# Interleaving the experts' hidden rows so that one gate tile serves a whole chunk, with new orders of work on every engine

## The chip, the cores and the metric

The kernel runs on one core of a Trainium2 chip. The time is the device time of one execution in microseconds (us). The kernel before was timed three times: 297.48, 299.65 and 299.68 us, median 299.65 us. The execution that the profiler recorded took 301.82 us, of which 300.0 us lie between the first and the last instruction.

## The reference, cut to what matters

There are 2048 tokens of 128 channels (4 batches of 512). Two layers follow each other, each a cross-attention and a feed-forward part, all with residuals. The first feed-forward part sends each token to one of 8 experts. The change lies in the second one, which computes every expert for every token:

```python
combine = zeros((n, E)).at[arange(n)[:, None], tidx].add(tw)   # n = 2048, E = 16, 4 of 16 are not zero
g = einsum('nh,eih->nei', x, w1)                  # I = 96 hidden values per expert
u = einsum('nh,eih->nei', x, w3)
hact = silu(g) * u * combine[:, :, None]          # the gate of a token and expert scales 96 hidden values
y = einsum('nei,ehi->nh', hact, w2)               # summed over experts and hidden values
shared = einsum('ni,hi->nh', silu(x @ ws1.T) * (x @ ws3.T), ws2)
return y + shared
```

The 16 x 96 = 1536 hidden values may stand in any order, as long as w1, w3, w2 and the gates use the same one.

## The kernel before, in words

Every engine walks its own list of stages, written out by hand in `ORDER`, an item `stage:n` at a time; semaphores between engines are the only other thing that sets the order. `a.` are the stages of the first attention and its router (chunks 0 to 3 of 512 tokens), `t.` the tiles of 128 tokens sorted by expert (11 tiles of the first group, chunk 0, then 19 of the second, chunks 1 to 3), `w.` the preparation of weights, and names without a prefix are the second attention and the second feed-forward part. `FILL` puts matmuls whose result nobody reads (`warm_b`, 512 columns) in front of some stages on PE.

The second feed-forward part works in blocks. For each of 4 chunks there are 13 blocks (`N1`), 12 of 128 hidden rows and one, the shared expert, of 96. `block(n)` maps the running number n to chunk c and block r; `SHARED` says at which r the shared expert stands. One block is:

- PE `g` and `u`: three 512-column matmuls each (high and low halves of a split product), into bank 0 and bank 1
- PE `e`: one matmul of the selection matrix `sel1` with the transposed gates `gT`, which spreads the 16 gates over the block's 128 hidden rows, into bank 3 (not for the shared block)
- ACT `silu` (L808) of bank 0 into `act`; DVE `prod` (L1300) act times bank 1; DVE `hm` (L1317) times bank 3 (the shared block takes bank 1 directly)
- ACT `high` (L814) rounds hm into `hring`; POOL `low` (L950) makes the remainder `lring`; PE `y` adds three matmuls to bank 2

`act`, `hm`, `hring` and `lring` have four places each. At the end of a chunk ACT `outcopy` takes bank 2 out, PE `oturn` transposes it, DVE `addout` adds it to x, and SP stores the chunk.

The gates of a chunk come from DVE `route0` to `route7`, some 35 small instructions on 128x64 values. `route7` writes gates as a high and a low half (L1272, L1274, L1275), PE `gturn` (L1615) transposes them to 32 rows, ACT `gcopy` (L802) writes them into `gT`. Both `gT` and `sel1` need zeros below row 32: POOL `clear` (L918, L919) writes them, after which ACT `sel` (L739) rounds `sel1` from a buffer that a DMA of 192 KB on ACT's queue filled at the start.

Between the sorted tiles and the blocks stand, for chunk 0: PE `wo`, DVE `add` with the statistics of the third norm, POOL `rstd3`, DVE `norm3`, PE `turn3`, PE `logit`, ACT `sg`, DVE `route`. For chunk 1 POOL `fetch:4` to `fetch:7` bring back the sorted rows by indirect DMA, then DVE `combine:1` with statistics, POOL `rstd2:1`, ACT `norm2:1`, PE `turn2:1`, `q:1`, `score:1`.

Of the kernel before, what the change touches and what calls it, by code (L numbers as in the profile page):

```python
# [1748 lines left out]
```

## Time and profile before

| | value |
|---|---|
| median of 3 runs | 299.65 us |
| profiled execution | 301.82 us, span 300.0 us |
| PE busy | 264.1 us (88%) |
| DVE, ACT, POOL busy | 192.8, 164.2, 151.6 us |
| mean granted TensorE clock | 0.975 |

A row of the timeline gives start and duration in us, the engine, the line, the operation with output and input tiles, and how many instructions are merged in it; in brackets is the idle time just before it and what ended it. Matmuls overlap, so the distance between two starts tells what one costs, not its duration. A row of the windows gives, for each engine, busy us and the number of instructions, then the granted clock.

### The profile page before, as it was taken

How to read it: one execution, taken by the hardware profiler on the slowest of the kernel's cores; microseconds unless marked ns; L12 is line 12 of the kernel's file. 1: busy time of each engine (PE TensorE's matmuls, PEld its weight loads, DVE VectorE, ACT ScalarE, POOL GpSimd, SP SyncE). 2: the span in 40 equal slices, each digit the busy share in tenths (PEclk: the TensorE clock that was granted, in tenths of full speed). 3: DMA queues.
4: the chain of work that ended last, by engine and by line, in shares of the span. 5: the costliest groups of instructions: out<-in, count | busy, mean ns of one | idle time of the engine just before them, and what ended most of it. 6: DMA issues, size and time to landing. Idle time of an engine off the chain costs nothing.

```text
span 300.0 us, 5426 instructions
## 1 busy us (share of the span) xinstructions
PE 264.1 (88%) x1712; PEld 197.4 (66%) x1719; DVE 192.8 (64%) x626; ACT 164.2 (55%) x325; POOL 151.6 (51%) x170
## 2 busy tenths in 40 slices
PE   8999966786679898649999999999899999999993
PEld 8787646675557654415667757776587876887871
DVE  5686655534284354696678888678695689755660
ACT  2745438352435740643866796677347864555441
POOL 2532876403259114854775923580556536655551
PEclk9999989799999999897999999999999999999999
DMA  7992262455553020100000000001000000000000
GB/s 240 363 378 118 86 218 74 112 137 148 154 138 93 19 63 9 28 9 16 27 13 9 2 0 2 2 0 37 0 2 1 1 35 2 1 0 35 2 1 35
DMA packets 19518, 19.60 MB, mean 65 GB/s; under 512 B 2194, under 2 KB 17154, under 8 KB 19234
## 3 DMA queue, kind: packets, MB, share of 16 engines
q1 hardware_dynamic: 13856, 14.41, 15.0%
q10 hardware_dynamic: 4610, 2.74, 3.1%
q0 software_dynamic: 1024, 2.10, 2.3%
q8 instruction: 14, 0.23, 0.3%
q14 instruction: 14, 0.11, 0.1%
HBM read 13.48 MB, written 5.77 MB: 64 GB/s over the span
## 4 chain that ended last, share of the span: by engine, by line
PE 39%; issue 23%; POOL 21%; DVE 10%; ACT 4%; another core or an unknown queue 1%; POOLq 1%; DVEq 0%; ACTq 0%
PE bank L1338 35%; POOL lring L950 11%; POOL gu1l L895 2%; PE bank L1350 2%; POOL rstd L855 2%; DVE sg L1222 1%; DVE st L974 1%; POOL rstd L850 1%; POOL w2l L901 1%; ACT xn L659 1%; DVE mpad L1186 1%; DVE xn L991 1%; ACT L808 1%; DVE x L1169 1%
## 5 line engine op out<-in xcount | busy, mean ns | idle before, releaser
L950 POOL TENSOR_TENSOR lring<-hm,hring 128x512 fp32r<-128x512 f32 (+1 forms) x52 | 66.5, 1290 | 63.1 <-ACT hring L814 63.1
L808 ACT ACTIVATE act<-bank 128x512 f32<-128x512 f32 (+1 forms) x52 | 31.0, 597 | 39.0 <-PE bank L1338 38.9
L1338 PE MATMUL bank<-xTh,gu1h 128*128 128x512 f32 (+1 forms) x104 | 45.2, 435 | 3.2 <-POOL xTl L861 2.5
L1300 DVE TENSOR_TENSOR act<-act,bank 128x512 f32<-128x512 f32 x48 | 32.9, 686 | 21.7 <-PE bank L1338 19.1
L1317 DVE TENSOR_TENSOR hm<-act,bank 128x512 f32<-128x512 f32 (+1 forms) x52 | 35.6, 684 | 12.9 <-PE bank L1338 9.3
L1338 PE MATMUL bank<-xTh,gu1l 128*128 128x512 f32 (+1 forms) x104 | 41.7, 401 | 0.0
L1338 PE MATMUL bank<-xTl,gu1h 128*128 128x512 f32 (+1 forms) x104 | 41.3, 397 | 0.0
L814 ACT CAST hring<-hm 128x512 fp32r<-128x512 f32 (+1 forms) x52 | 31.7, 617 | 10.6 <-DVE hm L1317 10.2
L747 ACT ACTIVATE hT<-bank,w 128x128 f32<-128x128 f32 x60 | 18.3, 364 | 22.3 <-PE bank L1338 22.0
L1338 PE MATMUL bank<-w,hT 128*128 x120 | 21.2, 301 | 10.6 <-DVE ys L1146 9.4
L1338 PEld LDWEIGHTS bank<-xTh,gu1h 128*128 128x128 f32 (+1 forms) x104 | 19.6, 189 | 13.8 <-issue 4.2
L659 ACT ACTIVATE xn<-x,shift_of,rstd 128x128 f32<-128x128 f32 x48 | 19.8, 483 | 14.9 <-POOL shift_of L857 14.9
L1338 PEld LDWEIGHTS bank<-w,hT 128*128 128x128 f32 x120 | 16.4, 198 | 16.2 <-issue 16.1
L1146 DVE TENSOR_TENSOR ys<-bank,b 128x128 f32<-128x128 f32 x30 | 8.7, 290 | 24.5 <-PE bank L1338 20.6
L1338 PEld LDWEIGHTS bank<-xTh,gu1l 128*128 128x128 f32 (+1 forms) x104 | 19.6, 188 | 4.9
L1338 PEld LDWEIGHTS bank<-xTl,gu1h 128*128 128x128 f32 (+1 forms) x104 | 19.8, 191 | 3.9 <-issue 0.6
L1338 PE MATMUL bank<-hring,w2h 128*128 128x512 f32 (+1 forms) x52 | 21.2, 407 | 1.0 <-POOL lring L950 1.0
L1338 PE MATMUL bank<-warm_b,onesb 128*128 128x512 bf16 x68 | 19.7, 381 | 1.6 <-issue 1.5
L1338 PE MATMUL bank<-hring,w2l 128*128 128x512 f32 (+1 forms) x52 | 20.5, 394 | 0.0
L1338 PE MATMUL bank<-lring,w2h 128*128 128x512 f32 (+1 forms) x52 | 20.4, 393 | 0.0
L1338 PE MATMUL bank<-xsT,w 128*128 128x128 f32 x120 | 19.6, 295 | 0.9 <-DVE xsT L1141 0.4
L1338 PE MATMUL bank<-gT,sel 128*128 128x512 f32 x48 | 19.5, 406 | 0.5 <-DVE hm L1317 0.4
(233 smaller groups left out, 522.6 us busy)
## 6 DMA issues: line engine op xcount, KB each, us to landing
w<-in_w SPq DMA_DIRECT2D x30, 129.0 KB
wf<-in_gu SPq DMA_DIRECT2D x1, 1632.0 KB, 9.3
xs<-sorted_x SPq DMA_DIRECT2D x19, 64.0 KB
sorted_y<-ys ACTq DMA_DIRECT2D x9, 128.0 KB, 2.1
x<-in_x SPq DMA_DIRECT2D x4, 256.0 KB, 5.2
w<-in_w SPq DMA_DIRECT2D x1, 1024.0 KB, 10.0
out_x<-x SPq DMA_DIRECT2D x4, 256.0 KB, 2.0
w<-in_w SPq DMA_DIRECT2D x1, 768.0 KB, 8.3
```

The lines of the kernel that those rows point to most:

```text
L659: nc.scalar.activation(normal(k, b)[:, j, :], x[:, b * TPB + j, :], ACT.Identity, bias=shift_of[:, ln(k, b), j:j + 1], scale=rstd[:, ln(k, ...
L747: last = nc.scalar.activation(hT0[:, t % 2, k, :], h_bank(t)[:, k * P:(k + 1) * P], ACT.Gelu, bias=b1_tile[:, t % SLOTS0, k:k + 1])
L808: nc.scalar.activation(act[0:m, n % 4, :], bank[0][0:m, :], ACT.Silu).then_inc(s.act_ready1, 1)
L814: nc.scalar.copy(hring[0:m, n % 4, :], hm[0:m, n % 4, :]).then_inc(s.hmh_ready, 1)
L855: nc.gpsimd.tensor_tensor(rstd[:, own, :], ve[:, own, :], mhalf[:, 0:TPB], ALU.pow).then_inc(s.ln_step[k], 1)
L895: nc.gpsimd.tensor_tensor(gu1l[:, w, own], gu1f[:, w, own], gu1h[:, w, own].bitcast(F32), ALU.subtract).then_inc(s.gul_ready, 1)
L950: nc.gpsimd.tensor_tensor(lring[0:m, n % 4, :], hm[0:m, n % 4, :], hring[0:m, n % 4, :].bitcast(F32), ALU.subtract).then_inc(s.hml_ready, 1)
L1146: nc.vector.tensor_tensor(ys[:, y_slot(t), :], y_bank(t)[:, 0:C], b2_0[:, bass.ds(own_expert[t], 1), :].rearrange("p o c -> p (o c)"), ALU ...
L1300: nc.vector.tensor_tensor(act[:, n % 4, :], act[:, n % 4, :], bank[1][:, :], ALU.mult).then_inc(s.prod_ready1, 1)
L1317: nc.vector.tensor_tensor(hm[0:m, n % 4, :], act[0:m, n % 4, :], bank[1 if r == SHARED[c] else 3][0:m, :], ALU.mult).then_inc(s.hm_ready1, 1)
L1338: return nc.tensor.matmul(dst, lhsT, rhs, start=start, stop=stop, skip_group_check=True)
L1350: last = nc.tensor.transpose(quarters(n)[:, j, :], normal(k, b)[:, j, :], ident)
```

## The change

The hidden rows of the 16 experts are interleaved on the host (`hidden`): block r now holds rows 8r to 8r+7 of every expert, so the gate of partition p is that of expert p // 8 in all 12 blocks. `route7` writes the gates of a chunk once, each repeated 8 times along the free axis (128x512), and `gturn` transposes that straight into bank 3, where it stays for the chunk. `sel1`, `gT`, the stages `e`, `gcopy`, `sel`, `clear` and the load of the selection matrix are gone. `gturn` of chunk n waits until all `hm` of the chunk before have read bank 3; the first `hm` with gates waits for it. The shared block comes first in every chunk. `oturn` moves from bank 3 to banks 2, 2, 4, 5, and where bank 2 is used the next chunk's first `y` also waits for `addout`. The statistics count one semaphore step instead of four. `t.h:11` waits for as many of the two late key products as stand up to `b.Vd`. SP's program has the same text and the same sequence as before: the second group's first five weight loads were already issued ahead of its rows.

```diff
-SHARED = (0, 4, 4, 4)
+SHARED = (0, 0, 0, 0)
...
-        "add:0 norm3:0 route0:0 combine:1 route1:0 route2:0 route3:0 route4:0 route5:0 route6:0 route7:0 hm:0 "
...
+        "add:0 norm3:0 route0:0 combine:1 hm:0 route1:0 route2:0 route3:0 prod:1 route4:0 route5:0 route6:0 "
...
+    "wo:0": 2,
+    "turn3:0": 12,
+    "logit:0": 2,
+    "g:0": 5,
+    "g:1": 3,
+    "u:1": 1,
+    "turn2:1": 6,
+    "q:1": 2,
...
-    "t.xs:11": 4,
-    "wo:0": 11,
-    "turn3:0": 15,
-    "logit:0": 2,
-    "g:0": 2,
-    "turn2:1": 8,
-    "score:1": 2,
...
-        gate1 = sb("gate1", [P, NT, 2, E1], F32R)
+        gate1 = sb("gate1", [P, TPB, E1, P // E1])
...
-        GATE_BANK = (3, 5, 5, 5)
+        OUT_BANK = (2, 2, 4, 5)
...
-            act_e.dma_start(sel1f, a["sel1"]).then_inc(s.ld_sel, 16)
...
-                elif stage == "clear":
-                    stored(NP)
-                    nc.gpsimd.memset(gT[:, :].bitcast(F32), 0.0).then_inc(s.cleared, 1)
-                    nc.gpsimd.memset(sel1[:, :, :].bitcast(F32), 0.0).then_inc(s.cleared, 1)
...
                 elif piece == 7:
-                    step(nc.vector.tensor_tensor(ra[:, t, :], ra[:, t, :], over(thr[:, t], E1), ALU.mult))
-                    step(nc.vector.tensor_copy(gate1[:, t, 0, :], ra[:, t, :]))
-                    nc.vector.tensor_tensor(gate1[:, t, 1, :], ra[:, t, :], gate1[:, t, 0, :].bitcast(F32),
-                                            ALU.subtract).then_inc(s.gate1_ready, 1)
+                    c = t0 // TPB
+                    if c:
+                        v.wait_ge(s.gT1_mm, c)
+                    nc.vector.tensor_tensor(gate1[:, :, :, :], ra[:, t, :].unsqueeze(3).broadcast_to([P, n, E1, P // E1]),
+                                            thr[:, t].unsqueeze(2).unsqueeze(3).broadcast_to([P, n, E1, P // E1]),
+                                            ALU.mult).then_inc(s.gate1_ready, 1)
...
                         v.wait_ge(s.prod_ready1, gated + 1)
-                        v.wait_ge(s.e_ready1, gated + 1)
+                        v.wait_ge(s.gT1_mm, c + 1)
...
-                        pe.wait_ge(s.kblk_ready, 2)
+                        pe.wait_ge(s.kblk_ready, [stage for stage, _ in order("DVE") if stage in ("b.Kd", "b.Vd")].index("b.Vd") + 1)
...
                     else:
-                        pe.wait_ge(s.at1_ready, 6 * min(n + 2, B))
+                        pe.wait_ge(s.hm_ready1, n * N1)
                     pe.wait_ge(s.gate1_ready, n + 1)
                     for j in range(TPB):
-                        last = nc.tensor.transpose(quarters(GATE_BANK[n])[0:2 * E1, j, :],
+                        last = nc.tensor.transpose(quarters(3)[:, j, :], gate1[:, j, :, :].rearrange("p e i -> p (e i)"), ident)
...
-                elif stage == "e":
...
-                    mm(bank[3][:, :], sel1[:, own, :], chunk(gT, c)).then_inc(s.e_ready1, 1)
...
                         pe.wait_ge(s.outT_ready, c)
+                        if OUT_BANK[c - 1] == 2:
+                            pe.wait_ge(s.o_added1, c)
...
+    def hidden(w):
+        return np.asarray(w).reshape(E1, R1, P // E1, C).transpose(1, 0, 2, 3).reshape(E1 * I1, C)
```

How the new tables move work is shown at three places. The first is PE where the sorted tiles end and the blocks begin, from `wo:0` (the first row with `aT`) on; `warm_b` rows are fills, `xTh` and `xTl` rows are `g` and `u`, `xn` rows transposes. Before:

```order
L1338 MATMUL bank<-warm_b,onesb 128x512 x11
L1338 MATMUL bank<-pack_b,aT 128x128 x4
L1338 MATMUL bank<-warm_b,onesb 128x512 x15
L1350 MATMUL bank<-pack_a,xn 128x128 x4
L1338 MATMUL bank<-warm_b,onesb 128x512 x2
L1338 MATMUL bank<-R1w,xT 128x128 x4
```

and after it, from the end of `g:1` to `u:1`:

```order
L1338 MATMUL bank<-warm_b,onesb 128x512 x8
L1350 MATMUL bank<-pack_a,xn 128x128 x4
L1338 MATMUL bank<-xT,pack_b 128x512
L1615 MATMUL bank<-pack_a,gate 32x128 x4
L1338 MATMUL bank<-xTh,gu1h 128x512
```

Now the same two pieces read:

```order
L1313 MATMUL bank<-warm_b,onesb 128x512 x2
L1313 MATMUL bank<-pack_b,aT 128x128 x4
L1313 MATMUL bank<-warm_b,onesb 128x512 x12
L1325 MATMUL bank<-pack_a,xn 128x128 x4
L1313 MATMUL bank<-warm_b,onesb 128x512 x2
L1313 MATMUL bank<-R1w,xT 128x128 x4
```

```order
L1313 MATMUL bank<-warm_b,onesb 128x512 x6
L1325 MATMUL bank<-pack_a,xn 128x128 x4
L1313 MATMUL bank<-warm_b,onesb 128x512 x2
L1313 MATMUL bank<-xT,pack_b 128x512
L1313 MATMUL bank<-xTh,gu1h 128x512
L1313 MATMUL bank<-xTl,gu1h 128x512
L1313 MATMUL bank<-xTh,gu1l 128x512
L1313 MATMUL bank<-maskrow,onesb 128x512 x4
L1313 MATMUL bank<-Kd,qT 128x128 x16
L1586 MATMUL bank<-pack_a,gate 128x128 x4
```

Nine of the 11 fills ahead of `wo:0` are gone. `u:1` now stands ahead of `turn2:1`, and `g:2` and `score:1` ahead of `gturn:0`.

The second place is POOL at the same time, after `rstd3:0` and the four fetches. Before:

```order
L873 DMA xn<-sorted_y,home 128x128 x4
L861 TENSOR_TENSOR xTl<-xT,xTh 128x512
L918 MEMSET gT 128x2048
L919 MEMSET sel 128x1536
L852 TENSOR_SCALAR ve<-mv 128x4
```

Now:

```order
L853 DMA xn<-sorted_y,home 128x128 x4
L841 TENSOR_TENSOR xTl<-xT,xTh 128x512
L832 TENSOR_SCALAR ve<-mv 128x4
L833 TENSOR_SCALAR nm<-mv 128x4
L835 TENSOR_TENSOR rstd<-ve,mhalf 128x4
```

The two memsets between `lowx:0` and `rstd2:1` are gone.

The third place is POOL in the first attention, behind `a.rstd2:0`. Before:

```order
L850 TENSOR_TENSOR rstd<-ve,mhalf 128x4
L852 TENSOR_SCALAR ve<-mv 128x4
L853 TENSOR_SCALAR nm<-mv 128x4
L855 TENSOR_TENSOR rstd<-ve,mhalf 128x4
L857 TENSOR_TENSOR shift_of<-nm,rstd 128x4
```

Now:

```order
L830 TENSOR_TENSOR rstd<-ve,mhalf 128x4
L900 TENSOR_SCALAR maskrow<-mask 128x512
L902 TENSOR_SCALAR keyoff<-maskT 128x4
L832 TENSOR_SCALAR ve<-mv 128x4
L833 TENSOR_SCALAR nm<-mv 128x4
```

`w.mask` came here from among the preparations of weights during the second group of tiles.

## Rows read from the trace of the kernel before

**Rows 1.** The page, busy time and share of the span of each engine.
```profile
PE 264.1 (88%) x1712; PEld 197.4 (66%) x1719; DVE 192.8 (64%) x626; ACT 164.2 (55%) x325; POOL 151.6 (51%) x170
```

**Rows 2.** Windows by stage: sorted tiles, first blocks, blocks beside attention, blocks alone.
```profile
44.00:110.00 66.00, 51.11 (x411) 41.42 (x410) 30.91 (x117) 34.79 (x87) 26.97 (x28) 0.96 0.39 109
124.00:138.00 14.00, 9.48 (x27) 4.69 (x29) 12.53 (x49) 5.65 (x10) 7.14 (x9) 0.76 0.04 11
138.00:250.00 112.00, 109.52 (x730) 79.80 (x729) 85.44 (x241) 75.92 (x133) 62.45 (x64) 1.00 0.03 9
250.00:290.00 40.00, 39.40 (x175) 31.15 (x173) 26.25 (x48) 20.11 (x35) 21.80 (x18) 1.00 0.02 7
```

**Rows 3.** Timeline, PE in the last chunk: from one block's g to the next.
```profile
279.00 0.40 PE L1338 MATMUL bank<-xTh,gu1h 128*128 128x512 f32 x1
279.69 0.39 PE L1338 MATMUL bank<-gT,sel 128*128 128x512 f32 x1
279.93 0.40 PE L1338 MATMUL bank<-xTh,gu1h 128*128 128x512 f32 x1
281.31 0.40 PE L1338 MATMUL bank<-xTh,gu1h 128*128 128x512 f32 x1
```

**Rows 4.** The page's costliest groups: busy us, mean ns of one, idle before, releaser.
```profile
L950 POOL TENSOR_TENSOR lring<-hm,hring 128x512 fp32r<-128x512 f32 (+1 forms) x52 | 66.5, 1290 | 63.1 <-ACT hring L814 63.1
L1300 DVE TENSOR_TENSOR act<-act,bank 128x512 f32<-128x512 f32 x48 | 32.9, 686 | 21.7 <-PE bank L1338 19.1
L1317 DVE TENSOR_TENSOR hm<-act,bank 128x512 f32<-128x512 f32 (+1 forms) x52 | 35.6, 684 | 12.9 <-PE bank L1338 9.3
L1338 PE MATMUL bank<-gT,sel 128*128 128x512 f32 x48 | 19.5, 406 | 0.5 <-DVE hm L1317 0.4
```

**Rows 5.** Timeline, passage: the end of the attention of chunk 0.
```profile
109.97 0.88 DVE L1204 TENSOR_TENSOR aT<-aT,bank 128x128 f32<-128x128 f32 x4
110.85 2.32 PE L1338 MATMUL bank<-warm_b,onesb 128*128 128x512 bf16 x10
113.01 1.05 PE L1338 MATMUL bank<-pack_b,aT 128*128 128x128 f32 x8
```

**Rows 6.** Timeline, first blocks: the last fetch, the clears, sg, combine, turn2.
```profile
121.57 0.94 POOL L873 DMA_INDIRECT xn<-sorted_y,home  x1 [0.30 <-issue]
122.90 4.03 DVE L1222 TENSOR_SCALAR sg<-sg 128x64 f32<-128x64 f32 x1 [4.13 <-issue]
123.73 1.83 POOL L918 MEMSET gT<- 128x2048 f32 x1
125.48 1.40 POOL L919 MEMSET sel<- 128x1536 f32 x1
127.81 1.14 DVE L1169 SCALAR_TENSOR_TENSOR x<-xn,score,x 128x128 f32<-128x128 f32 x4
133.00 1.39 PE L1350 MATMUL bank<-pack_a,xn 128*128 128x128 f32 x4 [3.43 <-ACT xn L659]
```

**Rows 7.** DMA issues: line engine op xcount, median us to landing.
```profile
xn<-first_sorted_y,slot POOLq DMA_INDIRECT x4, 2.9
```

**Rows 8.** Timeline, first blocks: first and last of route1 to route7.
```profile
130.19 0.16 DVE L1227 TENSOR_TENSOR pr<-sbs 128x32 f32<-128x32 f32 x1
136.67 0.22 DVE L1275 TENSOR_TENSOR gate<-route,gate 128x64 fp32r<-128x64 f32 x1
```

**Rows 9.** Timeline: a two-input DVE instruction beside POOL's low; the key product.
```profile
250.50 1.29 POOL L950 TENSOR_TENSOR lring<-hm,hring 128x512 fp32r<-128x512 f32 x1 [0.33 <-ACT hring L814]
250.55 1.32 DVE L1255 TENSOR_TENSOR route<-route,top 128x64 f32<-128x64 f32 x1
70.99 0.68 DVE L1154 TENSOR_TENSOR Kd<-kT,pack_b 128x512 f32<-128x512 f32 x1
```

**Rows 10.** Timeline: the same four norm instructions, POOL free and POOL busy.
```profile
20.91 1.11 DVE L991 TENSOR_SCALAR xn<-x,mv,rstd 128x128 f32<-128x128 f32 x4 [0.60 <-POOL rstd L850]
87.39 2.18 DVE L991 TENSOR_SCALAR xn<-x,mv,rstd 128x128 f32<-128x128 f32 x4
```

More of the change, by code:

```diff
@@ L162 @@
     "a.score:1": 1,
-    "a.own:0": 1,
     "a.wturn:0": 1,
@@ L167 @@
     "a.wturn:1": 1,
+    "a.turn:3": 1,
     "a.score:2": 1,
+    "a.turn2:0": 2,
     "a.own:1": 1,
+    "a.logit:0": 1,
     "a.mix:1": 1,
-    "a.turn2:0": 1,
     "a.wturn:2": 1,
-    "a.logit:0": 1,
+    "a.rank:0": 1,
     "a.own:2": 1,
-    "a.rank:0": 1,
+    "a.place:0": 1,
     "a.mix:2": 1,
-    "a.turn:3": 1,
-    "a.place:0": 1,
+    "a.score:3": 1,
     "a.turn2:1": 1,
-    "a.score:3": 1,
-    "a.logit:1": 1,
     "a.own:3": 1,
     "a.wturn:3": 1,
+    "a.logit:1": 1,
+    "a.mix:3": 1,
     "a.rank:1": 1,
-    "a.mix:3": 1,
-    "a.turn2:2": 2,
-    "a.logit:2": 3,
-    "t.xs:0": 2,
-    "t.xs:11": 4,
-    "wo:0": 11,
-    "turn3:0": 15,
-    "logit:0": 2,
-    "g:0": 2,
-    "turn2:1": 8,
-    "score:1": 2,
+    "a.turn2:2": 1,
+    "t.xs:0": 2,
+    "wo:0": 2,
[6 more added lines that the diff above has]
+    "q:1": 2,
+    "a.logit:2": 3,
 }
@@ L230, in xattn_moe_kernel @@
         xTl = sb("xTl", [C, NT * P], F32R)
-        gT = sb("gT", [P, NT * P], F32R)
-        sel1 = sb("sel1", [P, R1, P], F32R)
+        sb("early_only", [P, NT * P + R1 * P])
         (attn0, s0, kT0, vT0, A0, bqrep, aT0, V0, z0, m0, rk0, oh0, over0, past0, jump0, ones) = shared_room([
@@ L358, in xattn_moe_kernel @@
         hm = sb("hm", [P, 4, 512])
-        sel1f = hm[0:2 * E1, :, :].rearrange("p a n -> p (a n)")[:, 0:R1 * P].rearrange("p (r n) -> p r n", r=R1)
         outT = xT[:, 2, :]
@@ L372, in xattn_moe_kernel @@
         s.ld_tab = sem("ld_tab")
-        s.ld_sel = sem("ld_sel")
         s.ld_mask = sem("ld_mask")
@@ L401, in xattn_moe_kernel @@
         s.gul_ready = sem("gul_ready")
-        s.cleared = sem("cleared")
-        s.sel_ready = sem("sel_ready")
         s.s0_mm = sem("s0_mm")
@@ L476, in xattn_moe_kernel @@
         s.fetched0 = [sem(f"fetched_first{t}") for t in range(TPB - 1)]
-        s.ln_stats = [sem(f"ln_stats{k}") for k in range(4)]
         s.ln_var = [sem(f"ln_var{k}") for k in range(4)]
@@ L735, in weights @@
                     round_w2(n)
-                elif stage == "sel":
-                    act_e.wait_ge(s.ld_sel, 16)
-                    act_e.wait_ge(s.cleared, 2)
-                    nc.scalar.copy(sel1[0:2 * E1, :, :], sel1f).then_inc(s.sel_ready, 1)
             def sorted_tile(stage, t):
@@ L797, in stage1 @@
                     nc.scalar.activation(tiles(sg, n), tiles(sg, n), ACT.Exp, scale=-1.0).then_inc(s.sg_ready, 1)
-                elif stage == "gcopy":
-                    act_e.wait_ge(s.gT1_mm, n + 1)
-                    if n == 0:
-                        act_e.wait_ge(s.cleared, 1)
-                    nc.scalar.copy(chunk(gT, n)[0:2 * E1], bank[GATE_BANK[n]][0:2 * E1, :]).then_inc(s.gT1_ready, 1)
                 elif stage == "silu":
@@ L973, in statistics @@
                 for j in range(TPB):
-                    nc.vector.bn_stats(st[:, own, j, :], xc[:, j, :]).then_inc(s.ln_stats[k], 1)
-                v.wait_ge(s.ln_stats[k], TPB * (b + 1))
+                    last = nc.vector.bn_stats(st[:, own, j, :], xc[:, j, :])
+                step(last)
                 aggregate(k, b)
@@ L1172, in combine @@
                         v.wait_ge(s.x2_ready, t + 1)
-                        nc.vector.bn_stats(st[:, ln(2, 0), t, :], x[:, t, :]).then_inc(s.ln_stats[2], 1)
+                        last = nc.vector.bn_stats(st[:, ln(2, 0), t, :], x[:, t, :])
                 if b == 0:
-                    v.wait_ge(s.ln_stats[2], TPB)
+                    step(last)
                     aggregate(2, 0)
@@ L1308, in stage1 @@
                         v.wait_ge(s.hml_ready, n - 3)
-                    if n == 0:
-                        v.wait_ge(s.sel_ready, 1)
                     if r == SHARED[c]:
@@ L1320, in stage1 @@
                     v.wait_ge(s.out_mm, n + 1)
-                    nc.vector.tensor_tensor(tiles(x, n), tiles(x, n), quarters(3), ALU.add).then_inc(s.o_added1, 1)
+                    nc.vector.tensor_tensor(tiles(x, n), tiles(x, n), quarters(OUT_BANK[n]), ALU.add).then_inc(s.o_added1, 1)
             for stage, n in order("DVE"):
@@ L1543, in stage1 @@
                     pe.wait_ge(s.xT_ready[2], n + 1)
-                    if n == 3:
-                        pe.wait_ge(s.gT1_ready, 2)
                     mm(bank[5][:, :], attn1_w[:, 1, :], xT[:, xT_slot(2, n), :]).then_inc(s.q_mm, 1)
@@ L1637, in stage1 @@
                         .then_inc(s.u_mm if w else s.g_mm, 1)
-                elif stage == "e":
-                    c, r, own, m, gated = block(n)
-                    if gated == c * R1:
-                        pe.wait_ge(s.gT1_ready, c + 1)
-                    if gated == 0:
-                        pe.wait_ge(s.sel_ready, 1)
-                    else:
-                        pe.wait_ge(s.hm_ready1, n - 1 if r - 1 == SHARED[c] else n)
-                    if c and r == SHARED[c] + 1:
-                        pe.wait_ge(s.o_added1, c)
-                    mm(bank[3][:, :], sel1[:, own, :], chunk(gT, c)).then_inc(s.e_ready1, 1)
                 elif stage == "y":
@@ L1661, in stage1 @@
                     pe.wait_ge(s.outT_ready, n + 1)
-                    pe.wait_ge(s.hm_ready1, (n + 1) * N1 + SHARED[n + 1] if n < B - 1 else B * N1)
+                    if OUT_BANK[n] != 2:
+                        pe.wait_ge(s.at1_ready, 6 * B)
                     for j in range(TPB):
-                        last = nc.tensor.transpose(quarters(3)[:, j, :], cut(outT, j), ident)
+                        last = nc.tensor.transpose(quarters(OUT_BANK[n])[:, j, :], cut(outT, j), ident)
                     last.then_inc(s.out_mm, 1)
@@ L1731 @@
         "maskT": np.tile(np.asarray(mask_BxS2_bf0).T, (HG, 1)),
-        "sel1": np.tile(np.repeat(np.eye(E1, dtype=np.float32), I1, axis=1), (2, 1)).reshape(2 * E1, R1, P),
         "w1_0": np.concatenate([np.asarray(L0_ffn_W1), np.asarray(L0_ffn_b1).reshape(E0, HID0, P).transpose(0, 2, 1)], axis=2),
@@ L1735 @@
         "b2_0": np.asarray(L0_ffn_b2).reshape(1, E0, C),
-        "gu1": up(*(np.concatenate([np.asarray(w).reshape(E1 * I1, C), np.asarray(sw)]).T
+        "gu1": up(*(np.concatenate([hidden(w), np.asarray(sw)]).T
                     for w, sw in ((L1_ffn_w1, L1_ffn_ws1), (L1_ffn_w3, L1_ffn_ws3)))),
-        "w2_1": np.asarray(L1_ffn_w2).transpose(0, 2, 1).reshape(R1, P, C).transpose(1, 0, 2),
+        "w2_1": hidden(np.asarray(L1_ffn_w2).transpose(0, 2, 1)).reshape(R1, P, C).transpose(1, 0, 2),
         "ws2": np.asarray(L1_ffn_ws2).T,
```

5 lines of the change are left out of this document (removed), and 148 rows, old and new, of the table ORDER.

## The prediction

> **What bounds the kernel now.** I read the busy shares first: PE is busy 88% of the span, no other engine above 64% [rows 1]. An average hides stages, so the windows come next [rows 2]. From 138 to 250 us (blocks beside the second attention of chunks 1 to 3) and from 250 to 290 us (blocks alone) PE is busy 109.52 of 112 us and 39.40 of 40 us at full clock, DVE 85.4 and 26.3 us. In these 152 us what leaves PE shortens the run, as long as DVE, ACT and POOL keep up. The window before is another matter: from 124 to 138 us PE is busy 9.5 of 14 us, partly with fills, and the granted clock averages 0.76, so part of it ran at 1.2 instead of 2.4 GHz. From wo:0 to there the passage from sorted tiles to blocks is a chain through all engines, and its latency counts. From 44 to 110 us PE is busy 51 of 66 us; that stage waits from step to step.
>
> In the last chunk the same block returns every 281.31 - 279.00 = 2.31 us, ten matmuls, and `e` takes 279.93 - 279.69 = 0.24 us of it [rows 3]. Its listed 0.406 us [rows 4] contains the overlap with its neighbour and is not its price. The ten together give 0.231 us each, which I use.
>
> **The change, part by part.**
>
> 1. *48 `e` matmuls leave PE*: 48 x 0.231 = **-11.1 us**. A block falls to 2.08 us of PE. Against that stand per block on DVE 0.686 + 0.684 = 1.37 us and on POOL 1.29 us [rows 4]; both fit. The 16 transposes of the gates stay 16.
>
> 2. *Nine fills ahead of `wo:0` leave*. aT is complete at 110.85, just when the fills begin, and `wo` starts at 113.01; ten merged fills take 2.32 us, the last overlapping [rows 5]. The distance from 110.85 to 113.01 is 2.16 us for ten, 0.216 each, so nine give **-1.9 us**. DVE `add`, `norm3` and the fetches stand behind `wo`, so this passes on.
>
> 3. *The clears leave POOL*. DVE's first instruction on `sg`, of 64 columns, lasts 4.03 us, from 122.90 to 126.93; POOL's memsets run from 123.73 to 126.88, and `combine:1` starts at 127.81 [rows 6]. I read this as DVE held up by POOL's memory traffic. Without the memsets `combine:1` waits for its rows: the last fetch is issued at 121.57, and such a transfer lands 2.9 us after its issue where a row tells it [rows 7], at 124.5. That is 127.81 - 124.5 = **-3.3 us**. POOL is free earlier, which nobody waits for here. ACT loses the copies `sel` and `gcopy`; the nearest work, `combine:1` to `turn2:1` (127.81 to 133.00), does not wait for them, so nothing. The 192 KB load at the start counts nothing: its lower bound is 0, and at most it moves one queue entry.
>
> 4. *`u:1`, `g:2` and `score:1` ahead of `gturn:0`*. Before, all three stood behind the gates or right at them. The routing takes 136.89 - 130.19 = 6.7 us of DVE [rows 8]; now `hm:0` and `prod:1`, 0.69 us each, are laid into it, so with `combine:1` at 124.5 - 1.9 = 122.6 and 130.19 - 127.81 = 2.4 us until the routing goes on, gates come at 122.6 + 2.4 + 6.7 + 1.4 = 133.1. By then PE has done about 2.3 us of matmuls that stood behind the gates (two triples of 0.69 us, and of the score its four 512-column ones, 0.92 us). The shift at the gates is 136.9 - 133.1 = 3.8, plus 2.3 is 6.1 us, of which points 2 and 3 are 5.2. So **-0.9 us**.
>
> 5. *Two edits at the start of the second tile group*: four fills go (0.9 us) and the product Kd, 0.68 us [rows 9], is no longer waited for. **-1.5 us**. The new order of the tiles beyond that I take as nothing; PE's idle 15 us there [rows 2] bound it at -5, and at +3 for an order that fits worse.
>
> 6. *`w.mask` between two norms on POOL*. It runs where `a.norm2:0` does. The same four instructions took 1.11 us with POOL free and 2.18 us beside it [rows 10]: **+1.1 us**, between 0 and 1.5.
>
> 7. *One gate tile, one buffer*. `route7` becomes one instruction with two SBUF inputs and 512 columns. Such a one took 0.68 us [rows 9], the three small ones with their gaps 0.7 us: nothing. New is that `gturn` waits for the last `hm` of the chunk before and the first gated `hm` for `gturn`. The shared block in front (2.1 us of PE) and y blocks behind cover it; DVE has 0.7 us to spare per block. With banks 2 and 2 the first `y` of chunks 1 and 2 also waits for `oturn` and a 0.69 us `addout`; two or three stages of PE stand in between. I take **+1.0 us** for the three boundaries, between 0 and 5.
>
> A row speaks against this last point: beside a 1.29 us `low` of POOL a DVE instruction with two SBUF inputs took 1.32 instead of 0.22 us [rows 9]. Four gate instructions held up like that cost 4 x 1.1 = 4.4 us if each were on the path; that is in the upper bound of 5.
>
> The Trainium skill, "GPSIMD Engine Reference", section 8 "Key points", says that GpSimd shares its SBUF interfaces with VectorE, with contention for DVE instructions in a 2-port mode or with two SBUF inputs. By that rule the new gate instruction is exposed each time, and the clears were the cause of the 4.03 us; the trace agrees on both kinds of row, without showing which one yields.
>
> **Sum**: 301.8 - 11.1 - 1.9 - 3.3 - 0.9 - 1.5 + 1.1 + 1.0 = 285.2 us for a profiled execution. The profiled one of before stood 2.2 us above the median, so the forecast is **283.0 us**.
>
> **Rivals.**
>
> *The passage gives nothing* (chance 0.17). With 12 fewer fills PE may fall to 1.2 GHz for longer. It did so before, within 124 to 138 us; a 512-column matmul then costs twice 0.231 us, and 20 of them 4.6 us more; or the fetches land late. For it: the idle 4.5 of 14 us [rows 2]. Against: `u:1` and `g:2` now fill part of the hole. Points 2 to 4 vanish: 283.0 + 6.1 = 289.1 us.
>
> *DVE becomes the bound beside attention* (0.08). Its 85.4 us [rows 2] now lie in 112 - 34 x 0.231 = 104 us, 82%, with dependent small steps and hold-ups. If PE waits there for what it saved, 7.9 us return: 290.9 us.
>
> *The tiles gain more* (0.14). The tables are new for the first 110 us too, where PE idles more than 15 us. With 5 us from it: 278.0 us.
>
> *The single gate tile exposes the routing* (0.03), the one on the other side. If `route7` comes after the last `hm` of the chunk in each of the three boundaries and the routing is not overlapped, each stalls 6.7 us, 20 us in all: 283.0 - 1.0 + 20.1 = 302.1 us. It decides from (299.65 - 282.0) / 3 = 5.9 us a boundary on. Against it: `route0` to `route5` stand among the blocks of the chunk before.
>
> *Nothing changes in time* (0.02): `e` ran in a gap of PE anyway. Against it the 39.40 of 40 us.
>
> My forecast has the remaining 0.56, its own range being 279.5 to 286.5 us from points 5 to 7. The range to 8 in 10 goes down into the third rival and up to the first: 277 to 290 us. A change of 1% (3 us) is what a measurement here can tell; faster than 296.7 us are all but the last two rivals, 0.95; same 0.02, slower 0.03.
>
> **What would show it.** Blocks alone should return every 2.08 us. `sg` of chunk 0 should take under 0.6 us and `combine:1` start near 122.6. `wo:0` should start within 0.6 us of aT. The four norm instructions behind `a.rstd2:0` should show 2 us. From the passage to the end PE should stay above 96% busy. I am wrong if the block period stays above 2.2 us, if the window of the passage has a clock under 0.7, or if PE idles more than 3 us at a chunk's boundary.

## The result and the profile after

The changed kernel took 290.58 us, the median of four runs (287.22 to 293.30), beside 298.82 us of the kernel before on the same chip. The ratio is 0.964, with a 95% interval from 0.955 to 0.973: faster. This ratio, like every ratio below, leaves out the executions that took over 1.5% more than the shortest of their kernel, so it rests on 287.22 and 288.74 us here. The forecast was 283.0 us, in a range from 277 to 290: the sign is right, those two lie inside the range, 4 to 6 us above the forecast, and the median of all four lies 0.6 us above the range. The executions of the change fall into two groups about 5 us apart, which go with the granted clock: spans of 285.1 and 285.4 us at 0.96, and of 290.4 and 290.6 us at 0.94. The profile below is of the first group: 287.22 us, span 285.4, where the kernel before had 301.82 and 300.0. So the profiled gain is 14.6 us, where the working had 16.6.

The busy shares of the page answer to [rows 1], and the windows to [rows 2]:

```profile
PE 254.4 (89%) x1659; PEld 190.4 (67%) x1659; DVE 193.2 (68%) x618; ACT 158.5 (56%) x318; POOL 148.8 (52%) x168
```

```profile
44.00:110.00 66.00, 55.64 (x424) 45.68 (x423) 34.11 (x120) 31.71 (x83) 28.56 (x31) 0.89 0.39 106
119.00:133.00 14.00, 11.01 (x69) 5.62 (x71) 10.98 (x48) 8.03 (x14) 4.71 (x8) 1.00 0.06 14
133.00:240.00 107.00, 102.19 (x685) 73.65 (x679) 88.09 (x242) 74.64 (x131) 66.25 (x67) 1.00 0.04 11
240.00:275.00 35.00, 34.51 (x150) 26.98 (x149) 24.28 (x43) 19.78 (x36) 21.98 (x17) 1.00 0.00 1
```

The passage (119 to 133 us) has the full clock now; the kernel before had 0.76 in its window from 124 to 138 us, and 0.88 from 119 to 133 us. The tiles (44 to 110 us) have 0.89 against 0.96. Beside attention PE is busy 102.2 of 107 us, 95.5%, where it was 97.8%: PE has new gaps there.

The timeline of PE in the last chunk answers to [rows 3]; these are the first matmuls of `g` and `u` in turn:

```profile
261.94 0.40 PE L1313 MATMUL bank<-xTh,gu1h 128*128 128x512 f32 x1
262.64 0.40 PE L1313 MATMUL bank<-xTh,gu1h 128*128 128x512 f32 x1
264.03 0.40 PE L1313 MATMUL bank<-xTh,gu1h 128*128 128x512 f32 x1
264.72 0.40 PE L1313 MATMUL bank<-xTh,gu1h 128*128 128x512 f32 x1
266.11 0.40 PE L1313 MATMUL bank<-xTh,gu1h 128*128 128x512 f32 x1
```

From 261.94 over 264.03 to 266.11: a block every 2.08 to 2.09 us, as forecast. The passage, for [rows 5, 6]:

```profile
110.19 0.88 DVE L1180 TENSOR_TENSOR aT<-aT,bank 128x128 f32<-128x128 f32 x4
110.85 0.60 PE L1313 MATMUL bank<-warm_b,onesb 128*128 128x512 bf16 x2
111.28 1.06 PE L1313 MATMUL bank<-pack_b,aT 128*128 128x128 f32 x8
...
120.76 1.27 POOL L841 TENSOR_TENSOR xTl<-xT,xTh 128x512 fp32r<-128x512 f32 x1
121.13 0.95 DVE L1198 TENSOR_SCALAR sg<-sg 128x64 f32<-128x64 f32 x1 [4.13 <-ACT sg L782]
122.97 1.14 DVE L1145 SCALAR_TENSOR_TENSOR x<-xn,score,x 128x128 f32<-128x128 f32 x4
...
132.47 0.69 DVE L1251 TENSOR_TENSOR gate<-route,thr 128x512 f32<-128x512 f32 x1
132.70 1.60 POOL L926 TENSOR_TENSOR lring<-hm,hring 96x512 fp32r<-96x512 f32 x1 [5.23 <-ACT hring L794]
133.39 0.66 PE L1586 MATMUL bank<-pack_a,gate 128*128 128x128 f32 x4
```

`wo:0` starts 0.21 us after aT is complete (111.07), not 2.16. `sg` takes 0.95 us beside POOL's `lowx:0`, not 4.03. `combine:1` starts 11.69 us after `wo:0`, not 14.80. The new gate instruction takes 0.69 us, and 0.68 to 0.69 us in the other three chunks too. The next rows are the page's groups, for [rows 4]; the line of `e` is gone:

```profile
L926 POOL TENSOR_TENSOR lring<-hm,hring 128x512 fp32r<-128x512 f32 (+1 forms) x52 | 67.2, 1302 | 53.9 <-ACT hring L794 53.8
L1292 DVE TENSOR_TENSOR hm<-act,bank 128x512 f32<-128x512 f32 (+1 forms) x52 | 35.3, 685 | 3.7 <-POOL lring L926 0.4
```

Cut at the same landmarks, the two profiled executions differ so:

| stretch | before | after | difference | forecast |
|---|---|---|---|---|
| start to aT of chunk 0 complete | 110.85 | 111.07 | +0.2 | -0.4 |
| to `wo:0` | 2.16 | 0.21 | -1.95 | -1.9 |
| to `combine:1` | 14.80 | 11.69 | -3.1 | -3.3 |
| to `gturn:0` | 9.23 | 10.42 | +1.2 | +1.4 |
| to the end of the span | 162.96 | 152.01 | -10.95 | -12.4 |

The last two forecasts are point 4 (gates 10.5 us after `combine:1`, 2.3 us of matmuls taken out from behind them) with points 1 and 7. Two lines fail: 0.6 us at the tiles, 1.4 us in the blocks. The first is worse than it looks, since the profile of the kernel before has a wait of 2.69 us at 77.39 that the other does not have (last section). What the profile doesn't show is that the median lies 3.4 us over the profiled time. The experiments look for these.

### The profile page after: what moved, and what is told of

It is laid out like the page before. It is cut to its first block and busy times, and to the rows that moved or that the text cites. A ratio compares the mean times of both kernels' runs of the same rounds, so it can differ in the third digit from the quotient of the medians.

```text
span 285.4 us, 5281 instructions
## 1 busy us (share of the span) xinstructions
PE 254.4 (89%) x1659; PEld 190.4 (67%) x1659; DVE 193.2 (68%) x618; ACT 158.5 (56%) x318; POOL 148.8 (52%) x168
## 5 line engine op out<-in xcount | busy, mean ns | idle before, releaser
L926 POOL TENSOR_TENSOR lring<-hm,hring 128x512 fp32r<-128x512 f32 (+1 forms) x52 | 67.2, 1302 | 53.9 <-ACT hring L794 53.8
L1313 PE MATMUL bank<-xTh,gu1h 128*128 128x512 f32 (+1 forms) x104 | 44.6, 429 | 4.4 <-POOL xTl L841 1.8
L1277 DVE TENSOR_TENSOR act<-act,bank 128x512 f32<-128x512 f32 x48 | 32.8, 684 | 16.6 <-PE bank L1313 14.1
L1313 PE MATMUL bank<-xTh,gu1l 128*128 128x512 f32 (+1 forms) x104 | 41.1, 395 | 0.0
L1313 PE MATMUL bank<-hring,w2h 128*128 128x512 f32 (+1 forms) x52 | 22.0, 423 | 2.4 <-POOL lring L926 2.2
L1313 PEld LDWEIGHTS bank<-w,hT 128*128 128x128 f32 x120 | 16.6, 200 | 10.3 <-issue 10.0
L653 ACT COPY xT<-bank 128x512 f32<-128x512 f32 x16 | 9.3, 583 | 23.6 <-PE bank L1325 22.9
L1313 PE MATMUL bank<-warm_b,onesb 128*128 128x512 bf16 x63 | 20.7, 405 | 1.1 <-issue 1.1
L1313 PE MATMUL bank<-xsT,w 128*128 128x128 f32 x120 | 21.0, 306 | 0.1
```

The lines of the kernel that those rows point to most:

```text
L653: nc.scalar.copy(xT[:, xT_slot(k, b), :], bank[n][:, :]).then_inc(s.xT_ready[k], 1)
L926: nc.gpsimd.tensor_tensor(lring[0:m, n % 4, :], hm[0:m, n % 4, :], hring[0:m, n % 4, :].bitcast(F32), ALU.subtract).then_inc(s.hml_ready, 1)
L1277: nc.vector.tensor_tensor(act[:, n % 4, :], act[:, n % 4, :], bank[1][:, :], ALU.mult).then_inc(s.prod_ready1, 1)
L1313: return nc.tensor.matmul(dst, lhsT, rhs, start=start, stop=stop, skip_group_check=True)
```

## The experiments

In the text "old tables" stands for one variant used as a base: the changed kernel with each engine's table before `wo:0` (and its fills) taken from the kernel before. Runs 1 to 4 shared one chip, 5 to 8 a second, 9 to 12 the first again in another hour; the kernel before ran beside each (medians 299.74, 302.50, 302.28 us), so across groups ratios are compared.

**1. The change again.** No edit.

> The change, unaltered, beside its variants. Both theories of its scatter expect the spans of its executions in two groups about 5 us apart, near 285 us at a granted clock of 0.96 and near 290 us at 0.94. Theory A (the new orders for the sorted tiles leave TensorE at 1.2 GHz from 38 to 54 us, and in some executions longer) expects the longer executions to have their further loss in the first 110 us.

289.22 us (284.16 to 292.50); spans 282.2 and 283.5 us at 0.973 and 0.963, 290.7 and 290.6 at 0.937 and 0.939. The two groups come again, two executions each. The profiled one is 3.2 us shorter than that above, 1.9 of them gained before `wo:0` (109.41). The long ones were not profiled, so where they lose is not shown.

**2. Fills in the gaps.**

```diff
-    "a.turn2:0": 2,      "a.place:0": 1,   "a.own:3": 1,   "t.xs:0": 2,
+    "a.turn2:0": 6,      "a.place:0": 3,   "a.own:3": 3,   "t.xs:0": 6,
```

> The change with 12 more fills, all where TensorE waits in it: 4 ahead of a.turn2:0 (waits 0.89 us there), 2 each ahead of a.place:0 and a.own:3, 4 ahead of t.xs:0 (waits 1.09 us). Theory A (the clock is lost because TensorE has gaps between 20 and 40 us that the orders before did not have): the window 38 to 54 us has a clock above 0.9 instead of 0.5, tiles end 1 to 3 us earlier, the long executions vanish, best time 284 to 286, median 285 to 287 us. Theory B (the chain of DVE and POOL through the tiles sets their end, whatever the clock): same end of the tiles within 0.5 us, 287 us. Both: not slower, since the fills lie in idle time.

286.89 us (286.28 to 288.76), ratio 0.962 [0.956, 0.969]. None of the four executions is long: clocks 0.962 to 0.980, median 2.3 us down on the same chip. The shortest is 2.1 us longer than that of the change, and the timeline shows why:

```profile
41.66 2.72 PE L1313 MATMUL bank<-warm_b,onesb 128*128 128x512 bf16 x6 [1.23 <-issue]
44.18 0.37 PE L1475 MATMUL bank<-pack_a,xs 128*128 128x128 f32 x1
```

The granted clock is 0.50 from 41 to 44 us, that is 1.2 GHz; six fills take 2.5 us, and the first tile starts at 44.18 instead of 42.16. From 38 to 54 us the clock is 0.89, where the change had 0.50 in the profile above and 0.79 in run 1, so the fills did what theory A wanted of them. But the tiles do not end earlier: aT of chunk 0 is complete at 111.50, against 111.07 and 109.20. That is theory B's "same end within 0.5 us". What is left for theory A are the missing long executions, and four executions are few to tell that from chance. "Not slower, since the fills lie in idle time" was wrong: the gap was no longer idle once they ran late.

**3. Old tables.**

The cut is PE `wo:0`, DVE `add:0`, POOL `rstd3:0` (with `w.loww2:4` just ahead of it), ACT `unturn3:0`; `a.gain:3` on DVE and `a.pexp:3` on ACT, which the change had moved behind the cut, return ahead of it. Of POOL's table and of the fills for instance:

```diff
-"... a.rstd2:0 w.mask:0 a.rstd2:1 a.scatter:0 a.scatter:1 ..."
+"... a.rstd2:0 a.rstd2:1 w.r1:0 a.scatter:0 a.scatter:1 ..."
...
+    "t.xs:11": 4,
```

> The change with the part of each engine's table before wo:0 (DVE before add:0, POOL before rstd3:0, ACT before unturn3:0) and its fills taken from the kernel before; everything from the passage on is as changed. It tells what the new orders for attention and tiles are worth. Theory A (they lost by the clock what they won by order, point 5 of the prediction was offset): same best time within 1 us, 286.5 to 288, but no long executions, so a median 2 to 4 us lower than that of the change. Theory C (they gained the 1.5 us of point 5 less the 1.1 of point 6): 0.4 us slower. Theory D (the new orders simply are worse): 2 us faster in every execution.

283.11 us (282.65 to 283.99), ratio 0.948 [0.942, 0.954]: 6.1 us below the median of the change on the same chip. All four spans lie between 280.7 and 282.0 us. The means of like executions, 283.2 us here and 285.1 us for the shorter two of run 1, are 1.9 us apart, which is the 2 us that theory D named; the shortest fell by 1.5 us, where theory A allowed 1. The other 4 us of the median are the two long executions of run 1, of which there is no profile. **The new tables before `wo:0` cost 2 us against the shorter executions and 6 us in the median; all the rest of the change brings 16.6 us, to 283.1, where the forecast had 283.0.** Over all runs the ratios say the same: 0.956 to 0.964 for the change and its variants with new tables (runs 2, 4, 5, 10), 0.939 to 0.948 for the old tables (runs 3, 6, 9, 12), some 5 us between their middles.

The clock at 38 to 54 us does not explain it: it is 0.62 in this run's profile, lower than the 0.79 of run 1.

**4. The mask moved back on POOL.**

```diff
-"... a.rstd2:0 w.mask:0 a.rstd2:1 ..."
+"... a.rstd2:0 a.rstd2:1 ... w.loww2:2 w.mask:0 ..."
```

> The change with w.mask alone moved back on POOL, behind w.loww2:2 among the tiles. By point 6 of the prediction the four norm instructions behind a.rstd2:0 take 1.11 instead of 1.59 us again, and turn2 of chunk 0 starts 0.5 us earlier. Theory A (hold-up on the path): 0.5 to 1.0 us faster, 286.2 to 286.7 us. Rival (the path runs past it, through DVE's softmax of chunk 1): within 0.3 us of 287.2.

286.15 us (284.22 to 288.01), ratio 0.956 [0.947, 0.964]. In the timeline of the change, and then of this variant:

```profile
20.77 1.50 POOL L900 TENSOR_SCALAR maskrow<-mask 128x512 bf16<-128x512 uint8 x1
20.83 1.59 DVE L967 TENSOR_SCALAR xn<-x,mv,rstd 128x128 f32<-128x128 f32 x4 [1.12 <-POOL rstd L830]
```

```profile
20.82 1.12 DVE L967 TENSOR_SCALAR xn<-x,mv,rstd 128x128 f32<-128x128 f32 x4 [1.12 <-POOL rstd L830]
```

The hold-up is real and 0.5 us. DVE's `a.add:1` follows 0.5 us earlier (25.81 against 26.35), but `wo:0` does not (111.78, against 111.28 and 109.41 in the two profiles of the change). The shortest run is that of the change (284.22 against 284.16), and the shorter two of the change have a mean of 285.1 us, where the four here have 286.1: the rival. The median is 3.1 us lower only because no execution is above 288.01.

**5. POOL waits while DVE normalises.**

```diff
-"... rstd2:0 w.lowgu:1 w.lowgu:2 ... w.lowgu:7 bias1:0 ..."
+"... rstd2:0 bias1:0 w.lowgu:1 w.lowgu:2 ... w.lowgu:7 ..."
```

> The change with one item moved on POOL: bias1:0, which waits for the four norm instructions norm2:0 of the second layer's chunk 0, comes directly behind rstd2:0 instead of behind w.lowgu:7. So POOL waits while DVE does norm2:0, and w.lowgu:1 and 2 no longer run beside it. In the change norm2:0 takes 4.03 us there, and the tile copies xsT behind it on DVE wait. Theory E (POOL's splits hold DVE up, and this is where the new tile order loses its lead of 3.7 us over the old one): norm2:0 takes 1.1 us, the following t.xs:23 starts 2.9 us earlier, wo:0 1.5 to 3 us earlier, the run 1.5 to 3 us faster than the change (ratio to before 0.955). Rival (the weight splits that are delayed by 1.1 us on POOL, or the weight loads, set the end of the tiles): norm2:0 takes 1.1 us, but wo:0 moves by less than 0.5 us.

290.41 us beside 302.50, ratio 0.958 [0.951, 0.964]. The timeline of the change:

```profile
85.63 2.04 POOL L875 TENSOR_TENSOR gu1l<-wf,gu1h 128x408 fp32r<-128x408 f32 x2
85.68 4.03 DVE L967 TENSOR_SCALAR xn<-x,mv,rstd 128x128 f32<-128x128 f32 x4 [0.75 <-POOL rstd L830]
87.64 0.98 POOL L881 TENSOR_TENSOR w2l<-w,w2h 128x384 fp32r<-128x384 f32 x1
88.59 3.04 POOL L875 TENSOR_TENSOR gu1l<-wf,gu1h 128x408 fp32r<-128x408 f32 x3
89.83 0.28 DVE L1117 COPY xsT<-bank 128x128 f32<-128x128 f32 x1
90.25 0.30 PE L1475 MATMUL bank<-pack_a,xs 128*128 128x128 f32 x1 [0.16 <-DVE xsT L1117]
```

and of this variant:

```profile
90.58 1.12 DVE L967 TENSOR_SCALAR xn<-x,mv,rstd 128x128 f32<-128x128 f32 x4 [0.75 <-POOL rstd L830]
91.78 1.27 POOL L916 TENSOR_TENSOR x<-x,pack_b 128x512 f32<-128x512 f32 x1 [1.23 <-DVE xn L967]
```

norm2:0 takes 1.12 instead of 4.03 us, and from the tile before it (`t.xs:22`, 89.76) to `wo:0` (113.31) are 23.55 us, where run 1 has 26.45 (82.96 to 109.41): 2.9 us, all of it kept. Theory E holds for this stretch. The time does not show it: the ratio is that of the change, because `t.xs:22` comes at 89.76 here and at 82.96 to 85.30 in the four profiles of runs 1, 2, 4 and the change. Some 3 us of that are a wait at 57 to 61 us (last section); the rest is open, for the move itself lies behind that place in POOL's table. The stretch from `t.xs:22` to `wo:0` takes 26.4 to 27.2 us in those four, and 22.3 to 22.8 us in runs 3, 6, 8 and 9 with the old tables: the new order loses 4 us there, and 2.9 of them are this hold-up.

**6. The same move on the old tables.**

```diff
-"... rstd2:0 w.loww2:1 w.loww2:2 w.mask:0 ... bias1:0 ..."
+"... rstd2:0 bias1:0 w.loww2:1 w.loww2:2 w.mask:0 ..."
```

> The same move of bias1:0 in the variant whose tables up to wo:0 are the old ones (283.1 us median, norm2:0 2.14 us beside w2l). Theory E: norm2:0 takes 1.1 us, which is 1.0 us less; up to 1 us faster, 282.1 to 283.1 us. Rival: no difference, or up to 1 us slower since POOL's splits end later.

285.23 us beside 302.50, ratio 0.939 [0.932, 0.946]; the interval overlaps those of run 3 and run 9. The profile is of the longest execution (289.69 us). norm2:0 takes 1.11 us, but from `t.xs:22` to `wo:0` are 22.32 us against 22.48 in run 3: the rival. With the old tables the path does not run through norm2:0, though it takes 2.1 to 2.6 us there.

**7. The clears put back**, on the old tables, on a buffer that nobody reads.

```diff
+        "... fetch:7 lowx:0 w.clear:0 rstd2:1 ..."
...
+                elif stage == "clear":
+                    stored(NP)
+                    nc.gpsimd.memset(room[:, 0:NT * P].bitcast(F32), 0.0)
+                    nc.gpsimd.memset(room[:, NT * P:NT * P + R1 * P].bitcast(F32), 0.0)
```

> The variant with the old tables up to wo:0, plus POOL's two memsets (128x2048 and 128x1536) put back between lowx:0 and rstd2:1, on a buffer nobody reads. Point 3 of the prediction says that they held up DVE's sg by 3.3 us: sg of chunk 0 takes 4 us instead of 0.96, combine:1 starts 2.9 to 3.3 us later, 286.0 to 286.4 us. Rival (the fetches set combine:1, or the delay is caught up before the blocks): combine:1 less than 1 us later, 283.1 to 284.

291.01 us (288.42 to 293.03), ratio 0.957 [0.949, 0.964], 5.8 us above its neighbour, run 6. The profile is of the longest execution. Its timeline:

```profile
123.20 1.83 POOL L902 MEMSET early_only<- 128x2048 f32 x1
123.29 3.11 DVE L1204 TENSOR_SCALAR sg<-sg 128x64 f32<-128x64 f32 x1 [5.05 <-ACT sg L784]
124.95 1.40 POOL L903 MEMSET early_only<- 128x1536 f32 x1
127.28 0.88 DVE L1151 SCALAR_TENSOR_TENSOR x<-xn,score,x 128x128 f32<-128x128 f32 x3
```

From `wo:0` (112.47) to `combine:1` are 14.81 us, against 11.73 in run 3: 3.1 us, point 3. From there to the gates another 1.7 us are lost (12.10 against 10.42), which no theory had. The windows of this variant around the passage (PE busy, clock) show at what:

```profile
119.00:133.00 14.00, 9.71 (x33) 0.75 0.07 18
133.00:140.00 7.00, 6.91 (x56) 0.76 0.00 0
```

TensorE, with longer to wait, falls to 1.2 GHz just before the blocks. Run 9 (old tables) has 1.00 in both windows. Whether the shorter executions of this variant fall too is not shown.

**8. One more matmul in each gated block**, on the old tables.

```diff
                     w = 0 if stage == "g" else 1
+                    if w and r != SHARED[c]:
+                        mm(bank[1][:, :], gu1h[:, 1, rows], chunk(xTh, c))
```

> The variant with the old tables up to wo:0, plus one 512-column matmul ahead of u in each of the 48 gated blocks, whose result u overwrites. Point 1 of the prediction (TensorE sets the pace of the blocks): the block period in the last chunk goes from 2.08 to 2.31 us and the run is 48 x 0.231 = 11.1 us longer, 294.2 us. Rival (beside attention DVE, POOL or small waits hold PE back, so a matmul less or more is partly free there): the last chunk alone pays in full, 12 x 0.231 = 2.8 us, the rest less, 288 to 293 us.

293.41 us (292.98 to 294.57), ratio 0.969 [0.963, 0.974], 8.2 us above its neighbour, run 6; by the ratios it is 8 to 9 us above runs 9 and 6. Gates to end are 158.5 us against 150.5 in run 3, 8.0 us. In the last chunk POOL's `low` returns every 2.31 us (268.36, 270.68, 272.99), the full price. So **putting 48 matmuls back costs 8 us, not 11**: the rival. (It puts back the matmul alone, not `gcopy` on ACT nor the waits that `e` brought with it.) The rest goes into waits of PE beside attention. They show in the window from 140 to 240 us, of the old tables and of this variant:

```profile
140.00:240.00 100.00, 95.32 (x608) 1.00 0.03 9
```

```profile
140.00:240.00 100.00, 96.89 (x640) 1.00 0.03 9
```

Their releasers are in the waits of PE from 134 to 240 us, of the kernel before, then of the change:

```profile
PE bank L1338 <- DVE aT L1198: 1.7, 2, 1.5
PE bank L1338 <- ACT xT L664: 0.7, 1, 0.7
PE bank L1338 <- DVE hm L1317: 0.4, 1, 0.4
```

```profile
PE bank L1313 <- POOL lring L926: 1.4, 1, 1.4
PE bank L1313 <- DVE act L1277: 1.4, 3, 1.0
PE bank L1313 <- DVE aT L1174: 1.1, 2, 0.6
PE bank L1539 <- DVE mpad L1162: 0.6, 1, 0.6
```

2.8 us have become 4.5. With the matmul added to the old tables, the wait for `lring` falls from 1.4 to 0.6 us.

**9. Old tables, once more.**

> The variant with the old tables up to wo:0 once more, as the base for the three beside it: 283 us where the kernel before has 299.7, that is a ratio of 0.945.

285.62 us (283.46 to 287.03) beside 302.28, ratio 0.942 [0.937, 0.947].

**10. The new tables repaired**: 4 more fills ahead of `a.turn2:0`, 2 each ahead of `a.place:0` and `a.own:3`, and the move of run 5.

```diff
-    "a.turn2:0": 2,
-    "a.place:0": 1,
-    "a.own:3": 1,
+    "a.turn2:0": 6,
+    "a.place:0": 3,
+    "a.own:3": 3,
...
+"... rstd2:0 bias1:0 w.lowgu:1 w.lowgu:2 ..."
```

> The change with two repairs to its new order of the tiles and nothing taken back: fills where TensorE waits (4 more ahead of a.turn2:0, 2 each ahead of a.place:0 and a.own:3; none ahead of t.xs:0, where the 12-fill variant delayed the first tile by 2 us), and bias1:0 directly behind rstd2:0 on POOL, so that norm2:0 takes 1.1 instead of 4.0 us. Theory F (the new order for the tiles loses by these two and nothing else: TensorE at half clock, and DVE held up by POOL): as fast as the variant with the old tables within 1 us, and no execution above 287 us. Rival (the order itself loses it): norm2:0 at 1.1 us, but 3 us or more above the variant with the old tables.

291.07 us (289.80 to 292.43), ratio 0.962 [0.957, 0.967], 5.4 us above run 9. **Theory F falls.** norm2:0 takes 1.12 us, yet `wo:0` is at 113.18 against 110.88, and gates to end take 153.8 us against 151.9. The stretch from `t.xs:22` is as short as in run 5 (23.55 us), but `t.xs:22` is at 89.63, as late as there. The granted clock is 0.943 to 0.957 over the six runs, against 0.967 to 0.987 in run 9, though the fills of run 2 are in it, those ahead of `t.xs:0` apart; from 38 to 54 us it is 0.59, so the other eight fills do not hold it. Its windows where the blocks begin (PE busy, clock), then those of run 1:

```profile
145.00:150.00 5.00, 3.41 (x24) 1.00 0.10 26
150.00:155.00 5.00, 5.00 (x21) 0.66 0.06 13
175.00:180.00 5.00, 3.77 (x48) 1.00 0.00 0
180.00:185.00 5.00, 4.52 (x23) 0.66 0.02 3
```

```profile
145.00:150.00 5.00, 4.36 (x25) 1.00 0.05 13
150.00:155.00 5.00, 5.00 (x24) 1.00 0.05 13
```

Right behind a stretch in which PE waits, the clock falls: 0.66 over 5 us, that is some 3.4 us at the lower level. Such falls behind 145 us stand in the profiles of runs 4, 5, 6, 7, 9, 10 and 11, and not in the kernel before, nor in the change as profiled, nor in runs 1, 2, 3, 8 and 12. PE waits in those too (run 1: 3.46 of 5 us busy from 140 to 145; the change as profiled: 2.99 of 5 from 145 to 150), so a wait there makes a fall possible, not certain. An execution with one of them takes 151.7 to 152.3 us from gates to end, with two 153.6 to 153.8, against 150.5 to 152.0 without (run 8, with its added matmuls, left out).

**11. Eleven fills ahead of `wo:0`**, on the old tables.

```diff
-    "wo:0": 2,
+    "wo:0": 11,
```

> The variant with the old tables up to wo:0, with 11 fills ahead of wo:0 instead of 2, as in the kernel before. Point 2 of the prediction (they delay wo, and all behind it): wo:0 starts 1.9 us after its other matmuls are done instead of at once, 1.9 us slower. Rival (they keep the clock up, so that what they cost comes back behind them): less than 0.7 us slower, with a clock of 1.00 in the passage against 0.9.

288.49 us (286.79 to 290.20), ratio 0.953 [0.947, 0.958], 2.9 us above run 9, where 1.9 was expected. aT is complete at 111.03 and `wo:0` starts at 113.19: 2.16 us against 0.22. From `wo:0` to the end are 174.2 us against 174.1. Nothing is given back; the passage has the full clock in both. The rival falls, and point 2 stands.

**12. `low:2` ahead of `rstd2:2` on POOL**, on the old tables.

```diff
-"... fetch:13 rstd2:2 low:2 low:3 ..."
+"... fetch:13 low:2 rstd2:2 low:3 ..."
```

> The variant with the old tables up to wo:0 and low:2 ahead of rstd2:2 on POOL. In it and in the change TensorE waits 1.40 us for lring ahead of y:2, while POOL does the statistics of chunk 2 first; xn of that chunk is ready 3 us before TensorE takes it. If this wait is real and the matmuls beside attention are what sets the end: 1 to 1.4 us faster, 281.6 to 282.1. Rival (the wait moves to the next of DVE's or ACT's steps): no difference.

285.84 us (283.81 to 287.75), ratio 0.943 [0.938, 0.948]: no difference. The wait for `lring` falls from 1.4 to 0.2 us, and one for ACT's `act` stands in its place:

```profile
PE bank L1315 <- ACT act L790: 1.7, 1, 1.7
```

So the start of the blocks is bound by the chain through DVE, ACT and POOL: relieving one place in it brought no time. No variant beats the old tables by more than the runs can tell; they are the best kernel here, 0.942 to 0.948 of the time before.

## Why the prediction was right or wrong

**The sign and the bulk were right, the total in part by luck.** Points 1 to 4 were to bring 17.2 us, and old tables with everything else changed are 16.6 us faster than before. But inside that sum the errors cancel. From the gates to the end run 3 takes 150.52 us, 12.4 less than the kernel before, and the forecast had 12.4 (11.1 + 2.3 - 1.0). Of these, run 8 finds 8.0 us for the matmuls, not 11.1; what point 4 takes out from behind the gates is 3.8 us, not 2.3; point 7's loss of 1.0 does not show; and 0.6 us are left.

*Point 1* was right in its mechanism and in the price of a matmul (block 2.31 to 2.08 us), and mis-sized in its sum: 48 x 0.231 = 11.1 us holds where PE is 98% busy by itself, in the blocks alone. There the 12 matmuls of the last chunk cost 2.8 us; the other 36, beside attention, cost 5.2 us where 8.3 were forecast. The rival "DVE becomes the bound beside attention" described this and priced it at the whole; about 3 us of it came, and the releasers are DVE, ACT and POOL in turn.

*Point 2*: -1.95 in the trace, 1.94 (2.16 - 0.22) in that of run 11, whose medians lie 2.9 us apart. Right.

*Point 3*: -3.1, by removing and by putting back. Right, for the reason given. That a longer wait also costs the clock at the first blocks (run 7, 1.7 us more in the one execution profiled) was missing.

*Point 4*: gates 10.42 us after `combine:1`, forecast 10.5. Right; `u:1`, `g:2` and `score:1` fill the hole, and the clock of the passage is 1.00 (0.95 in run 1). What stood behind the gates was underpriced. In the kernel before, from `gturn:0` to `u:2`:

```profile
137.04 1.01 PE L1615 MATMUL bank<-pack_a,gate 128*32 128x128 f32 x4
141.28 0.39 PE L1338 MATMUL bank<-xTh,gu1h 128*128 128x512 f32 x1
```

That is 4.24 us, and 0.41 in the change (133.39 to 133.80). The difference of 3.8 us holds the whole score, two fills ahead of it, and the clock, which was 0.50 from 137 to 138 us.

*Point 5* **is the step that failed**, in its sentence "The new order of the tiles beyond that I take as nothing", with a bound of +3. It cost 2 us against the shorter executions and about 6 us in the median. Its first part was too high as well: in the kernel before PE waited only 0.3 us for `Kd` (what the four fills were worth was not tried). What the runs show of the loss: the new order runs the first group of tiles ahead (`t.xs:11` at 66.35 against 70.30 in runs 1 and 3) and loses that lead in the second, 4.0 us of it from `t.xs:22` to `wo:0`. There 2.9 us are norm2:0 laid beside POOL's weight splits, since moving one item brings them back (run 5); the other 1.1 us were not separated. Why the median loses 4 us more is not shown. Neither run 2 nor run 4 had an execution at 0.94, but with four executions each that can be chance, and run 2's own test of the clock failed. Both repairs together did not close the gap (run 10), in part by a wait that only the profiles of runs 5 and 10 have, so most of the 6 us stays open.

*Point 6*: norm2 of the first attention took 1.59 instead of 1.11 us: +0.5, forecast +1.1, and `wo:0` did not move by it. Inside its bounds.

*Point 7*: no boundary stalls over 1.0 us. The gate instruction was held up in no chunk (0.68 to 0.69 us in all four), so the 4.4 us that spoke against this point did not come. In chunk 0 POOL's remainder, which started 0.23 us after it, took 1.60 us, where such instructions take 1.30 in the mean. Whether the single gate tile costs anything was not tried by itself; its +1.0 can't be told from the waits of point 1.

Of what was named as telling signs, the block period, `wo:0`, `combine:1` (0.4 us late), the clock of the passage and the boundaries came out as said. `sg` took 0.95 us beside POOL's `lowx:0`, and 0.56 in run 1, where under 0.6 was forecast; the four norm instructions took 1.59, not 2 us. From 133 to 275 us PE is busy 96.3%, just above the 96% named, and 95.5% beside attention.

## What to carry to other kernels

In this kernel the price of an instruction taken from the busiest engine counted in full only where that engine waited for nothing by itself; elsewhere put an instruction back and measure what it costs. A total that comes out right proves none of its terms: cut the profile at the same landmarks and compare term by term. A new order for a stage that the edit does not touch is a change of its own: cost it at its bounds, not at nothing, and time it apart. When work is taken away, look for the gaps it leaves, since behind each some 3.4 us may run at the lower TensorE clock.
